# Fewer VectorE operations and more small matmuls in the expert routing of a two-layer model

## The reference, cut to what matters

```
logits = xn @ gate_w.T                       # 8 numbers for each token
probs = softmax(logits); tk_probs, tk_idx = top_k(probs, 2)
tk_probs = tk_probs / (sum(tk_probs) + EPS)
out = swiglu_shared(x) + sum over the two experts e of w[e] * swiglu_e(x)     # layer 0
topv, topi = top_k(x @ Wgate + bgate, 2); topw = softmax(topv)               # layer 1
y = sum over the two experts of topw * expert(x)
```

## Time and profile before

| what | value |
|---|---|
| median of 3 runs | 1265.88 us (1260.65 to 1266.71) |
| the profiled execution, its own time | 1259.49 us |
| its span | 1257.7 us |
| PE busy | 1116.6 us (89%) |
| DVE busy | 836.8 us (67%) |
| POOL busy | 602.6 us (48%) |
| ACT busy | 504.9 us (40%) |
| mean granted PE clock | 0.955 |
| chain that ended last | PE 44%, DVE 6%, issue 4% |

### The profile page before, as it was taken

How to read it: one execution, slowest core, us unless ns; L and a number is a source line. 1 busy time by engine, 2 the same in 40 slices (tenths; PEclk the granted TensorE clock), 3 DMA queues, 4 the chain that set the end, 5 groups by cost and what they waited for, 6 DMA issues and landing times.

```text
span 1257.7 us, 24179 instructions
## 1 busy us (share of the span) xinstructions
PE 1116.6 (89%) x8163; PEld 758.8 (60%) x8163; DVE 836.8 (67%) x2229; ACT 504.9 (40%) x1147; POOL 602.6 (48%) x701
## 2 busy tenths in 40 slices
PE   6768788876789898899999999999979699999998
PEld 3445555555348887344455454454444699999993
DVE  4769788888434444436769878787786366666664
ACT  3335344443304444034444444444431344544540
POOL 1456688888634555332255455552445133333330
PEclk9889899998879999989999999999999899999999
DMA  4987887663123532211012011110111411111105
GB/s 130 258 196 170 228 222 177 162 165 106 35 64 106 160 104 57 67 37 47 10 51 60 27 52 58 37 33 21 47 37 49 150 40 45 38 40 44 38 22 207
DMA packets 87314, 113.09 MB, mean 90 GB/s; under 512 B 11224, under 2 KB 68888, under 8 KB 84616
## 3 DMA queue, kind: packets, MB, share of 16 engines
q1 hardware_dynamic: 68120, 86.35, 25.5%
q0 software_dynamic: 8640, 17.84, 4.4%
q10 hardware_dynamic: 10432, 7.35, 2.3%
HBM read 81.06 MB, written 32.04 MB: 90 GB/s over the span
## 4 chain that ended last, share of the span: by engine, by line
PE 44%; DVE 6%; issue 4%; ACT 2%; POOL 1%; DVEq 1%; SPq 1%; DMA 1%; another core or an unknown queue 0%; ACTq 0%; POOLq 0%
PE bank L2132 8%; PE bank L2234 4%; PE bank L2121 4%; PE bank L1884 3%; PE bank L2246 3%; PE bank L2296 2%; PE bank L2327 2%; PE bank L2297 2%; PE bank L2316 2%; PE bank L2148 2%; PE bank L2342 1%; DVE rows L1036 1%; PE bank L2312 1%; PE bank L2360 1%; PE bank L2344 1%
## 5 line engine op out<-in xcount | busy, mean ns | idle before, releaser
L1274 POOL DMA_INDIRECT slots<-pay,slot x128 | 129.4, 1011 | 114.2 <-issue 92.6
L2121 PE MATMUL bank<-rows,wup 128*128 128x128 f32 x1136 | 155.0, 281 | 15.4 <-DVE wup L761 13.9
L1289 POOL DMA_INDIRECT y<-region,xin x78 | 84.2, 1080 | 149.3 <-ACT region L1693 132.7
L2121 PEld LDWEIGHTS bank<-rows,wup 128*128 128x128 f32 x1136 | 141.0, 195 | 19.6 <-DVE rows L749 9.8
L2132 PE MATMUL bank<-rows,wse 128*128 128x128 f32 x1136 | 141.6, 278 | 1.7 <-DVE wse L766 1.7
L1793 ACT ACTIVATE w0uv<-bank 128x512 f32<-128x512 f32 x192 | 99.6, 603 | 99.9 <-PE bank L2297 53.0
L2132 PEld LDWEIGHTS bank<-rows,wse 128*128 128x128 f32 x1136 | 132.3, 192 | 7.5 <-issue 6.6
L1884 PE MATMUL bank<-consts 128*128 128x512 f32 x240 | 119.0, 634 | 2.0 <-DVE region L1058 2.0
L1289 POOL DMA_INDIRECT y<-hh,region x64 | 69.0, 1078 | 100.2 <-ACT hh L1693 91.3
L1036 DVE TENSOR_REDUCE rows<-bank 128x4 f32<-128x512 f32 x128 | 80.1, 683 | 41.4 <-PE bank L2234 36.9
L754 DVE SCALAR_TENSOR_TENSOR rows<-bank,bcol,rows 128x128 f32<-128x128 f32 x142 | 43.4, 347 | 92.9 <-ACT rows L1682 92.8
(11 more groups left out here) (373 smaller groups left out, 2326.7 us busy)
## 6 DMA issues: line engine op xcount, KB each, us to landing
region<-vrdram SPq DMA_DIRECT2D x16, 1024.0 KB
region<-vrdram SPq DMA_DIRECT2D x32, 512.0 KB, 9.8
xin<-slots SPq DMA_DIRECT2D x78, 65.0 KB
region<-slots SPq DMA_DIRECT2D x64, 65.0 KB
wgl<-in_wgl SPq DMA_DIRECT2D x8, 512.0 KB
rows<-y SPq DMA_DIRECT2D x8, 512.0 KB, 4.2
wam<-xres SPq DMA_DIRECT2D x9, 256.0 KB, 2.9
xres<-wam SPq DMA_DIRECT2D x9, 256.0 KB, 2.3
```

Of the source, the lines that this page charges most:

```text
L1274: p.indirect_dma_start(io["slots"], bass.IndirectOffsetOnAxis(ap=slot_of(l, b)[:, k, t:t + 1], axis=0), pay_of(l, b)[:, k, t, :], None).th ...
L1289: p.indirect_dma_start(io["y"], bass.IndirectOffsetOnAxis(ap=xins[par][:, h, k, P + 1:P + 2].bitcast(U32), axis=0), bYs[par][:, h, k, :], ...
L2121: ins = M(bank_up(l, n)[:, tile(j)], wup[:, n % 3, tile(j)], bxT[:, q % 2, tile(k)], start=True, stop=True)
```

## The change

`rank` gives the ranks over the whole batch and one total for each expert: the triangle's matmul is followed by three matmuls with the square of ones that add the tiles ahead (24, 16 and 8 columns) into the same place in PSUM, and four matmuls of 8 columns add up the total. That is 8 matmuls in place of 2. `base` shrinks to one row of 8 numbers. On DVE the two comparisons become one over 64 elements, `place` has 5 operations in place of 12 and layer 1's `weights` 5 in place of 6; the last operation of `place` is a maximum that writes `slot` directly as whole numbers. The destination numbers are worked out from the constants with the batch's number.

```diff
-                for k in range(2):
-                    link(V.tensor_tensor(oh[:, k, :, :], bc(iota, NT, 1), bc(idxf[:, :, k], E, 2), ALU.is_equal))
+                link(V.tensor_tensor(oh[:, :, :, :], bc(bc(iota, NT, 1), 2, 1), bc(idxf[:, :, 0:2].rearrange("p t k -> p k t"), E, 3), ALU.is_equal))
...
-                link(V.reciprocal(rsm[:, 2, :], rsm[:, 1, :]))
-                link(V.tensor_tensor(rsm[:, 3, :], rsm[:, 2, :], ex[:, :, 1], ALU.mult))
-
-                link(V.tensor_copy(pay_of(layer, b)[:, :, :, P].rearrange("p k t -> p k t"), rsm[:, 2:4, :]))
+                pay = pay_of(layer, b)
+                link(V.reciprocal(pay[:, 0, :, P], rsm[:, 1, :]))
+                link(V.tensor_tensor(pay[:, 1, :, P], pay[:, 0, :, P], ex[:, :, 1], ALU.mult))
...
-                link(V.tensor_copy(pay_of(layer, b)[:, :, :, P + 1].bitcast(U32), dcur[:, :, :]))
-                link(V.tensor_scalar(dcur[:, :, :], dcur[:, :, :], 2.0 * T, None, ALU.add))
+                link(V.tensor_scalar(pay_of(layer, b)[:, :, :, P + 1].bitcast(U32), consts[:, C_DST:C_DST + 2 * NT].rearrange("p (k t) -> p k t", k=2), 2.0 * T * b, None, ALU.add))
                 v.wait_ge(S["q_p"], b + layer * NB + 1)
-                for t in range(NT):
-                    link(V.tensor_tensor(base[:, t + 1, :], base[:, t, :], totals[:, t, :], ALU.add))
-                link(V.tensor_tensor(pos[:, :, :], ranks, base[:, 0:NT, :], ALU.add))
-                link(V.tensor_copy(base[:, 0, :], base[:, NT, :]))
-                for k in range(2):
-                    link(V.tensor_tensor(oh[:, k, :, :], oh[:, k, :, :], pos[:, :, :], ALU.mult))
-                link(V.tensor_reduce(slotf[:, :, :].rearrange("p k t -> p (k t)"), oh[:, :, :, :].rearrange("p k t e -> p (k t) e"),
-                                     axis=AX, op=ALU.add))
+                link(V.tensor_tensor(pos[:, :, :], ranks, bc(base[:, :], NT, 1), ALU.add))
+                link(V.tensor_tensor(base[:, :], base[:, :], total, ALU.add))
+                assert n[0] == Q_READ
+                link(V.tensor_tensor(oh[:, :, :, :], oh[:, :, :, :], bc(pos[:, :, :], 2, 1), ALU.mult))
                 assert n[0] + 1 == Q_STEPS
-                link(V.tensor_copy(slot_of(layer, b)[:, :, :], slotf[:, :, :]))
+                link(V.tensor_reduce(slot_of(layer, b)[:, :, :].rearrange("p k t -> p (k t)"), oh[:, :, :, :].rearrange("p k t e -> p (k t) e"),
+                                     axis=AX, op=ALU.max))
...
-                M(route_bank(l, b)[:, 64:64 + NT * E], consts[:, C_TRI:C_TRI + P], ms, start=True, stop=True)
-                M(route_bank(l, b)[:, 128:128 + NT * E], consts[:, C_ONE:C_ONE + P], ms, start=True, stop=True).then_inc(S["q_p"], 1)
+                tri, ones = consts[:, C_TRI:C_TRI + P], consts[:, C_ONE:C_ONE + P]
+                ranks, total = route_bank(l, b)[:, 64:64 + NT * E], route_bank(l, b)[:, 128:128 + E]
+                M(ranks, tri, ms, start=True, stop=False)
+                for s in range(1, NT):
+                    M(ranks[:, s * E:NT * E], ones, ms[:, 0:(NT - s) * E], start=False, stop=s == NT - 1)
+                for t in range(NT):
+                    ins = M(total, ones, ms[:, t * E:(t + 1) * E], start=t == 0, stop=t == NT - 1)
+                ins.then_inc(S["q_p"], 1)
```

More of the change, by code:

```diff
@@ L179, in build @@
         msum = sb("msum", [P, NT, E])
-        base = sb("base", [P, NT + 1, E])
+        base = sb("base", [P, E])
         pos = sb("pos", [P, NT, E])
-        slotf = sb("slotf", [P, 2, NT])
         slotss = sb("slot", [P, 2, NT], U32), sb("slot1", [P, 2, NT], U32)
-        dcur = sb("dcur", [P, 2, NT])
         tnb = sb("tnb", [1, 3, E])
@@ L224, in build @@
         S = Semaphores()
-        R_STEPS = (18, 18)
+        R_STEPS = (17, 16)
         ex_p = bank[6][:, 192:192 + NT * E].rearrange("p (t e) -> p t e", e=E)
@@ L291, in build @@
         SCAT = 2 * NT * 16
-        TAB_STEPS, Q_STEPS, MOD_STEPS = 17, 12, 6
+        TAB_STEPS, Q_STEPS, Q_READ, MOD_STEPS = 17, 5, 3, 6
         SCALE = float(DH) ** -0.5
@@ L630, in router @@
                 if half == 1:
-                    n[0] = R_STEPS[layer] - (5 if layer == 0 else 6)
+                    n[0] = R_STEPS[layer] - 5
                     (weights_first if layer == 0 else weights)(layer, b, eps, link)
@@ L650, in router @@
                 link(V.tensor_copy(idxf[:, :, :], idx[:, :, :]))
-                for k in range(2):
-                    link(V.tensor_tensor(oh[:, k, :, :], bc(iota, NT, 1), bc(idxf[:, :, k], E, 2), ALU.is_equal))
+                link(V.tensor_tensor(oh[:, :, :, :], bc(bc(iota, NT, 1), 2, 1), bc(idxf[:, :, 0:2].rearrange("p t k -> p k t"), E, 3), ALU.is_equal))
                 V.tensor_tensor(msum[:, :, :], oh[:, 0, :, :], oh[:, 1, :, :], ALU.add).then_inc(S["q_m"], 1)
-                assert n[0] == R_STEPS[layer] - (5 if layer == 0 else 6), n[0]
+                assert n[0] == R_STEPS[layer] - 5, n[0]
             def weights_first(layer, b, eps, link):
@@ L687, in place @@
                 ranks = route_bank(layer, b)[:, 64:64 + NT * E].rearrange("p (t e) -> p t e", e=E)
-                totals = route_bank(layer, b)[:, 128:128 + NT * E].rearrange("p (t e) -> p t e", e=E)
-                link(V.tensor_copy(pay_of(layer, b)[:, :, :, P + 1].bitcast(U32), dcur[:, :, :]))
-                link(V.tensor_scalar(dcur[:, :, :], dcur[:, :, :], 2.0 * T, None, ALU.add))
+                total = route_bank(layer, b)[:, 128:128 + E]
+                link(V.tensor_scalar(pay_of(layer, b)[:, :, :, P + 1].bitcast(U32), consts[:, C_DST:C_DST + 2 * NT].rearrange("p (k t) -> p k t", k=2), 2.0 * T * b, None, ALU.add))
                 v.wait_ge(S["q_p"], b + layer * NB + 1)
-                for t in range(NT):
-                    link(V.tensor_tensor(base[:, t + 1, :], base[:, t, :], totals[:, t, :], ALU.add))
-                link(V.tensor_tensor(pos[:, :, :], ranks, base[:, 0:NT, :], ALU.add))
-                link(V.tensor_copy(base[:, 0, :], base[:, NT, :]))
-                for k in range(2):
-                    link(V.tensor_tensor(oh[:, k, :, :], oh[:, k, :, :], pos[:, :, :], ALU.mult))
-                link(V.tensor_reduce(slotf[:, :, :].rearrange("p k t -> p (k t)"), oh[:, :, :, :].rearrange("p k t e -> p (k t) e"),
-                                     axis=AX, op=ALU.add))
+                link(V.tensor_tensor(pos[:, :, :], ranks, bc(base[:, :], NT, 1), ALU.add))
+                link(V.tensor_tensor(base[:, :], base[:, :], total, ALU.add))
+                assert n[0] == Q_READ
+                link(V.tensor_tensor(oh[:, :, :, :], oh[:, :, :, :], bc(pos[:, :, :], 2, 1), ALU.mult))
                 assert n[0] + 1 == Q_STEPS
-                link(V.tensor_copy(slot_of(layer, b)[:, :, :], slotf[:, :, :]))
+                link(V.tensor_reduce(slot_of(layer, b)[:, :, :].rearrange("p k t -> p (k t)"), oh[:, :, :, :].rearrange("p k t e -> p (k t) e"),
+                                     axis=AX, op=ALU.max))
             def start_counts():
-                V.tensor_copy(base[:, 0, :], consts[:, C_BASE:C_BASE + E]).then_inc(S["prep_q"], 1)
-                V.tensor_copy(dcur[:, :, :].rearrange("p k t -> p (k t)"), consts[:, C_DST:C_DST + 2 * NT]).then_inc(S["prep_q"], 1)
+                V.tensor_copy(base[:, :], consts[:, C_BASE:C_BASE + E]).then_inc(S["prep_q"], 1)
             def tables(layer):
@@ L719, in tables @@
                 ej, sj, rj, mj = (tf[:, i, :] for i in range(4))
-                link(V.tensor_copy(padrow[:, :], base[0:1, 0, :]))
-                link(V.tensor_tensor(nbf, base[0:1, 0, :], consts[0:1, C_BASE:C_BASE + E], ALU.subtract))
+                link(V.tensor_copy(padrow[:, :], base[0:1, :]))
+                link(V.tensor_tensor(nbf, base[0:1, :], consts[0:1, C_BASE:C_BASE + E], ALU.subtract))
                 link(V.tensor_scalar(tnbi[:, :], nbf, P - 1.0, None, ALU.add))
@@ L856, in prepare_rest @@
                 start_counts()
-                v.wait_ge(S["prep_q"], 2)
+                v.wait_ge(S["prep_q"], 1)
             def mod_rows():
@@ L1009, in _ @@
             start_counts()
-            v.wait_ge(S["prep_q"], 4)
+            v.wait_ge(S["prep_q"], 2)
             experts(0)
@@ L2038, in first_logits @@
                 if b:
-                    t_.wait_ge(S["q_f"], (b - 1) * Q_STEPS + NT + 3)
+                    t_.wait_ge(S["q_f"], (b - 1) * Q_STEPS + Q_READ)
                 else:
@@ L2202, in placed @@
             def placed(b):
-                return (b + NB) * Q_STEPS + NT + 3
+                return (b + NB) * Q_STEPS + Q_READ
             def local_values(b, p):
```

## The result

The changed kernel takes 1295.49 us (1292.82 to 1304.37, 4 runs) against 1266.3 us for the one before (1260.65 to 1268.09, 4 runs). The ratio is 1.025, 95% interval 1.022 to 1.028. The forecast was 1268 us with a range up to 1277, so it was wrong: the change makes the kernel slower by 29 us. The profiled execution of the changed kernel took 1292.93 us with a span of 1291.1, 33.4 us longer than the span of before. A time given as 1.011 is the ratio to the kernel before, run in the same group, and the numbers in brackets behind it are its 95% interval.

The account below looks back on a forecast made before the run. It took layer 0's recurrence as a ring with no engine full and layer 1's attention as bound by PE. -6.3 + 1.3 + 6.0 + 1.4 = +2.4 us, on the median of 1265.88, gave 1268 us, range 1256 to 1277.

Parts of the forecast that it names:

- Prices on DVE: Routing on DVE, both layers: 1.57 us saved a batch in layer 0, 1.77 in layer 1, 26.7 us in all.
- Price of a rank on PE: Rank's matmuls on PE: six more at 0.23 us cost 1.38 us a batch, 22 us over 16 batches.
- PE's 1.38 costs nothing here: Layer 0: PE's added time is covered by DVE's work; DVE waited in only 2 places, 3.5 us together.
- the ring: Layer 0's recurrence through several engines: an earlier slot gives 0.9 us for each of 7 batches, -6.3 us (0 to -11.0).
- Last batch of layer 0: Layer 0's last batch, at half clock with nothing beside it: +2.65 - 1.37 = +1.3 us.
- Layer 1, steady steps: Layer 1, steps 3 to 7: PE's added time mostly passes, 1.2 us for each of five ranks, +6.0 us.
- rival B: 25%: the stall takes up PE's time in layer 1, steady steps -0.8 in place of +6.0; 1261.5 us.
- is worth nothing there: Layer 1's steady steps: DVE's saving gains nothing because DVE waits about 2 us for PE behind place.
- The clock: Sign of being wrong: the granted clock of layer 1's tail moving with the added matmuls; no size given.
- Tail: Layer 1's end, last ranks, filling and last batch: +1.4 us (-1 to +3).
- A: Likeliest rival, 45%: the sum as forecast, near 1264 to 1272 us with its bounds.
- C: 17%: layer 0 gains nothing as the next batch's load sets its pace, PE's time passes in full; +9.6, 1275.5 us.

Follow-up runs that it names:

- e15: Kernel before with six more matmuls of 8 columns behind rank's two, in layer 0 alone, output unread; 1.0065 (1.004 to 1.009).
- e18: Kernel before with the change in layer 0 alone and two-byte ranks in both layers; 0.995 (0.992 to 0.997), 1259.18 us against 1266.49.
- e12: Kernel before with the change's savings on DVE, the old two rank matmuls, and layer 1's scatters split four and four; 1.0005.
- e10: Kernel before, run again unchanged for a profile; 1.0006 of before, median 1258.1 us.
- e1: Kernel before with the whole change in layer 0 alone, layer 1's routing as before; 1.0054 (1.0019 to 1.0088).
- e16: Changed kernel with msum, triangle and ones at two bytes an element; 1.010 (1.008 to 1.013).
- e17: Changed kernel with two-byte ranks and layer 1's eight scatters split into four and four; 0.997 (0.995 to 0.999).
- e14: Changed kernel with three more filling matmuls ahead of the second global scores in layer 1's routing steps; 1.017 (1.011 to 1.022).
- e11: Changed kernel with layer 1's eight scatters split into four and four; 1.012 (1.005 to 1.019), median 1276.0 us.
- e9: Changed kernel, run again beside the kernel before; 1.024 (1.020 to 1.029), median 1290.1 us.
- e13: Changed kernel with POOL's difference moved ahead of layer 1's eight scatters; 1.040 (1.034 to 1.046).
- e5 to e8: One group: changed with split scatters 1.011, before with split 1.0004, changed with difference first 1.008, changed with more filling matmuls 1.014; before at 1224.97 us.

## Why the prediction was wrong, step by step

- **Prices on DVE: right in sum.** 25.8 us saved against 26.7; a 64-element operation 0.22 where 0.20 to 0.45 was the bound; place took 1.11 us where it waits for nothing (950.19 to 951.30). But the product over 64 elements took 0.74 to 0.94 in three batches of layer 0, one of the text's own signs of being wrong, and beside POOL before's place was long in four batches, not in the one row that the text knew of.
- **Price of a rank on PE: right.** +1.32 against +1.38 us, and 1.3 us a step in the group without waits. Accumulating into one place shows no cost of its own: 0.22 us a matmul, where the logits' take 0.23.
- **"PE's 1.38 costs nothing here" (layer 0): the first step that failed.** It rested on a count of waits, 3.5 us at 2 places. That counts where DVE was late already, not how much room it had elsewhere. In 4 of the ring's 7 batches the room did not suffice, and the text had named waits in more than two places as a sign that would make it wrong. The wait for `q_p` stands ahead of unit 6 in the ring. The price of losing the cover was in the text, 1.38 a batch, 11 us over eight, and no rival carried it. Measured: e15, with only that added, +8 us. With the price taken away e18 is 7 us below before, which agrees with the -6.3 for the ring but does not prove it: PE's cheaper ranks may have up to some 4 of the 7 us, and e12, whose place is 6 us shorter in layer 0 than e10's (18.0 for 24.3 us over eight batches) with PE's work as before, gains nothing in all. As written, the sum had -5.0 for layer 0; e1 measured +7. How much of that passes through the waits for the ranks stays open: the experts start at 369.8 to 381.0 us in nine profiles with the changed layer 0 at 372.0 to 377.7 in five with that of before, and at 367.8, 374.3 and 368.6 in e16, e17 and e18, whose layer 0 is the same.
- **Last batch of layer 0:** forecast +1.3; from its rank to its scatter the changed kernel takes 353.35 - 346.86 = 6.5 us, before 5.4, so +1.1. Right.
- **Layer 1, steady steps: the second step that failed, and the larger.** The forecast had +1.2 a step or, in rival B, PE's time absorbed in the stall. Both took the stall at POOL's line 1413 as something of fixed length. It is not: whatever waits for PE on ACT or DVE can be held while POOL is in the second half of eight scatters and up to 1.7 us beyond it, and which of PE's results fall into that time depends on both engines. PE's lead over the scatters fell from 3.57 to 1.9 us, 1.3 of it by PE and 0.3 by DVE, and ACT's copy of the local values and its third exponentials then fell into that time. The steps grew by 4.5 us in place of 1.2. The sentence that DVE's saving "is worth nothing there" was wrong in sign in these steps: in e16, with no price left on PE, they are 3.6 us longer than e15's.
- **The clock.** The text names a clock that moves as a way to be wrong only for the tail. PE's added idle time lies in the steady steps, where the clock falls from 0.97 to 0.92; e14, which fills that time, gets about 10 us back.
- **Tail:** forecast +1.4, with step 7's own rank +2.6. From the last step's start to the experts it is 97.9 us in e10, 101.8 in e11 and 108.5 in e9, so about +4 with split scatters and +11 with eight in a row; the changed kernel's first profile has +7.9 over before's.
- **Rivals.** A and C had PE's time pass as it is, B had it vanish; the measured time is 18 us above the end of the range. Rival C was on the right side by the wrong mechanism. A's range of 1264 to 1272 is also narrower than the bounds it names: their high ends, 0 + 1.3 + 5 x 1.8 + 3, add up to +13.3 or about 1279. The rule cited with B ("PE and ACT never wait on anyone", the Trainium skill, "SBUF — State Buffer", "Who interferes with whom") speaks of ports, and no run here shows a port holding ACT; I let it count against any hold of POOL over ACT. e13 shows such a hold of 7.5 us.

What stays open: by what path eight scatters in a row delay the news of PE's results, and why one group of runs had none of it. That group's experts of layer 0 were faster too, 151.4 us between 372 and 523 where before has 174.4. The chip with number 1 showed both, in e5 to e8 and in e17 and e18. The lead over the scatters orders the kernels roughly, but no run changed it alone, and no experiment took the scatters themselves away.

## What to carry to other kernels

Before work is moved to an engine because "it waits there in only two places", read how much room each of the other places has: a count of waits says nothing of it. A stall whose end coincides with another engine's row of DMAs is not a buffer that absorbs delay; moving either end by a microsecond can put other work under it, and the added idle time can go together with a lower clock of PE. Small whole numbers can go through PE at two bytes an element: here that made eight matmuls cheaper than two.

## What the hardware showed unexpectedly

- While POOL issues eight indirect DMAs 1.26 us apart, ACT and DVE start on PE's results up to 7.5 us late (e13), mostly 0.7 to 4.2 us, and no such wait ends before 6.4 us after the first of them; with four in a row and then a gap, 3 us or less in most steps and up to 4.8. In one group of runs it did not happen at all.
- Eight matmuls of 8 to 32 columns take 1.78 us at four bytes (2 records each, 0.22 us a matmul) and 0.28 us at two bytes (1 record each, 0.035 us).
- A DVE product over 128x64 elements takes 0.22 us, and 0.74 to 0.94 in the three batches in which it starts inside POOL's operation on 128x512; 8-element copies and conversions of the kernel before took 0.81 to 1.05 in place of 0.17 us in the same way.
